# Three stages of a fused kernel: self attention with its products in another order, single-head attention with query and key on ScalarE, contexts in 128 rows

## What is computed

```python
x = x + L0_xattn(layernorm(x), ctx)     # 16 heads, cross
x = x + L0_ffn(layernorm(x))            # 8 experts, top 1
x = x + L1_xattn(layernorm(x), ctx)     # one head of width 128, cross
x = x + L1_ffn(layernorm(x))            # 15 experts, top 3, and a shared one
x = x + L2_xattn(layernorm(x), ctx, mask)   # 16 heads, masked
x = x + L2_ffn(layernorm(x))            # a whole block: causal self attention, then 8 experts
x = x + L3_xattn(layernorm(x), ctx)     # 8 heads of width 64
x = x + L3_ffn(layernorm(x))            # 8 experts with a capacity
```

```python
query = x @ Wq + bq; key = ctx @ Wk + bk; value = ctx @ Wv + bv
attended = softmax(query @ key.T / sqrt(128)) @ value
```

```python
q = rmsnorm(apply_rope(q, cos, sin), qn_w)      # the rms of 20 heads of 8
attn = softmax(where(causal, q @ k.T / sqrt(8), -inf)); out = attn @ v
out = out * sigmoid(out @ Wg + bg);  x = x + out @ Wo + bo
```

## Times and profile before

| | |
|---|---|
| median of 3 runs | 1868.89 us (1868.3 to 1873.9) |
| profiled execution | 1870.34 us, span 1868.5 us |
| mean granted TensorE clock | 0.909 of full speed |
| TensorE busy | 1506.6 us, 81% of the span |
| VectorE busy | 1329.3 us, 71% |
| ScalarE busy | 959.9 us, 51% |
| GpSimd busy | 860.5 us, 46% |

### The profile page before, as it was taken

How to read it: one execution, slowest core, us unless ns; L and a number is a source line. 1 busy time by engine, 2 the same in 40 slices (tenths; PEclk the granted TensorE clock), 3 DMA queues, 4 the chain that set the end, 5 groups by cost and what they waited for, 6 DMA issues and landing times. The chain is left out here.

```text
span 1868.5 us, 37548 instructions
## 1 busy us (share of the span) xinstructions
PE 1506.6 (81%) x11614; PEld 1169.2 (63%) x11614; DVE 1329.3 (71%) x4215; ACT 959.9 (51%) x1953; POOL 860.5 (46%) x1432
## 2 busy tenths in 40 slices
PE   5999949877898989788885888888768899999840
PEld 3666639865687777455553555555557798888630
DVE  4899943278777777688875888888556688887522
ACT  2788825433343333477773777777533344444310
POOL 2456643355110010233326777888544555665426
PEclk9999969978899999699985999999879899999965
DMA  6776118511000000000000000000066000000043
GB/s 200 234 267 236 36 36 258 161 39 33 5 1 1 1 1 1 7 9 9 9 2 1 1 2 1 6 7 8 16 182 198 14 15 13 21 21 18 12 149 89
DMA packets 60786, 108.35 MB, mean 58 GB/s; under 512 B 11715, under 2 KB 49620, under 8 KB 59796
## 3 DMA queue, kind: packets, MB, share of 16 engines
q1 hardware_dynamic: 54452, 93.45, 16.1%
q0 software_dynamic: 6144, 12.60, 2.3%
HBM read 89.49 MB, written 52.17 MB: 76 GB/s over the span
## 5 line engine op out<-in xcount | busy, mean ns | idle before, releaser
L716 DVE TENSOR_REDUCE parts<-PS 128x8 fp32r<-128x1024 f32 x192 | 234.1, 1219 | 42.4 <-PE PS L463 38.0
L954 ACT ACTIVATE P<-PS 128x1024 f32<-128x1024 f32 x192 | 198.3, 1033 | 71.7 <-PE PS L478 71.6
L931 ACT CAST qS<-PS 32x512 fp32r<-32x512 f32 x384 | 221.2, 576 | 6.8 <-PE PS L430 3.5
L1788 DVE SCALAR_TENSOR_TENSOR X<-PS,wt,X 128x128 f32 (+1 forms) x480 | 134.4, 344 | 49.5 <-PE PS L1631 40.9
L279 POOL TENSOR_TENSOR ve<-mv,eps_t 128x1 f32<-128x1 f32 x160 | 31.9, 199 | 283.3 <-DVE mv L275 282.9
L1920 ACT ACTIVATE P<-PS,w_f_b 128x512 f32<-128x512 f32 x128 | 88.0, 688 | 142.7 <-PE PS L1612 141.2
L1631 PEld LDWEIGHTS PS<-w_f_w,P 128*128 128x128 f32 x1024 | 130.4, 193 | 39.8 <-issue 27.9
L1631 PE MATMUL PS<-w_f_w,P 128*128 128x128 f32 x1024 | 142.4, 283 | 13.7 <-DVE X L1788 11.9
L478 PE MATMUL PS<-qS,kS 128*128 128x512 f32 x384 | 149.3, 444 | 1.0 <-ACT P L954 1.0
L430 PE MATMUL PS<-ident_r,parts 128*128 128x128 f32 x768 | 124.3, 293 | 30.7 <-issue 25.2
L845 POOL TENSOR_TENSOR rrs<-rsq,neg_half 128x20 f32<-128x20 f32 x32 | 115.2, 3600 | 46.4 <-DVE rsq L646 45.9
(11 more groups left out here) (302 smaller groups left out, 4332.4 us busy)
## 6 DMA issues: line engine op xcount, KB each, us to landing
P<-in_f_blob SPq DMA_DIRECT2D x12, 578.0 KB, 4.4
Y<-in_f_blob SPq DMA_DIRECT2D x11, 578.0 KB, 4.4
ctxT<-in_ctxT SPq DMA_DIRECT2D x128, 48.0 KB, 1.8
tok<-hs SPq DMA_DIRECT2D x46, 128.0 KB, 3.3
hs<-yo SPq DMA_DIRECT2D x46, 128.0 KB, 3.7
P<-in_f_blob SPq DMA_DIRECT2D x12, 450.0 KB, 4.3
Y<-in_f_blob SPq DMA_DIRECT2D x11, 450.0 KB, 4.7
w_f_w<-in_f_w SPq DMA_DIRECT2D x2, 1024.0 KB, 5.6
```

What stands on the lines that cost most here:

```text
L716: e.tensor_reduce(parts[:, it.s, 0, 8 * half:8 * half + 8, 3, 0], S_ps[:, :, :].rearrange("p i (j t) -> p (i j) t", t=T), AXX, ALU.max)\
L931: m = e.copy(qS[r, it.s % 2, :, j, :], TP[0][r, :].rearrange("p (g t) -> p g t", g=4))
L954: e.activation(P[:, it.s % 2, 8 * half:8 * half + 8, :].rearrange("p h t -> p (h t)"), ST_ps[:, :, :].rearrange("p j n -> p (j n)"), ACT.E ...
L1788: m = e.scalar_tensor_tensor(out=X_s, in0=rows, scalar=wt[:, b, s, x:x + 1], in1=X_s, op0=ALU.mult, op1=ALU.add)
```

## The change

Three edits stand together.

1. In the self attention VectorE does `v_heads` and `v_heads_back` ahead of `v_qk_norm`, and TensorE's order is `pe_stack_k`, `pe_scores(0)`, `pe_stack_q`.
2. In the single-head attention query and key leave PSUM on ScalarE (`a_qk`, at the head of its tick), the value alone on VectorE (`v_v`), from a bank of its own pair; `pe_qkv` waits for both, and GpSimd issues its gathers three ahead.
3. The context tile and the six context weights get 128 rows, of which the last 32 are zero (one memset of the tile, the weights padded on the host); the DMAs fill the first 96 rows of the tile as before.

```diff
-        weight("a1", "a1_wk", [C, D])
+        weight("a1", "a1_wk", [128, D])
...
-        ctxT = sb("ctxT", [C, RING, T])
+        ctxT = sb("ctxT", [128, RING, T])
...
-                        e.dma_start(ctxT[:, s, :], ctx_dram[:, 0, s, :]).then_inc(s_ctx[s], 16)
+                        e.dma_start(ctxT[0:C, s, :], ctx_dram[:, 0, s, :]).then_inc(s_ctx[s], 16)
...
                         if it := item(L + 1):
-                            pe_stack_q(e, it)
                             pe_stack_k(e, it)
                         if it := item(L):
                             pe_scores(e, it, 0)
+                        if it := item(L + 1):
+                            pe_stack_q(e, it)
...
-                        if it := item(F + 1):
-                            v_qk_norm(e, it)
                         if it := item(L + 3):
                             v_heads(e, it)
                             v_heads_back(e, it)
+                        if it := item(F + 1):
+                            v_qk_norm(e, it)
...
-            QKV = [FR, PS[:, 3, :]]
+            QK = [FR, PS[:, 3, :]]
+            V = [PS[:, 1, :], PS[:, 5, :]]
...
                     if due(it.n - 1):
                         e.wait_ge(s_v, at(s_v, it.n - 1))
-                    bank = QKV[it.s % 2]
+                        e.wait_ge(s_qk, at(s_qk, 2 * (it.n - 1)))
+                    bank = QK[it.s % 2]
...
-                    e.tensor_scalar(q1[:, it.s, :], bank[:, 0:T], w[p + "bq"][:, 0:1], None, ALU.add).then_inc(s_qk, 1)
-                    e.tensor_scalar(k1[:, it.s, :], bank[:, T:2 * T], w[p + "bk"][:, 0:1], None, ALU.add)\
-                     .then_inc(s_qk, 1)
-                    e.tensor_tensor(v1[:, it.s, :], bank[:, 2 * T:3 * T], w[p + "bv"][:, :], ALU.add).then_inc(s_v, 1)
+                    e.tensor_tensor(v1[:, it.s, :], V[it.s % 2][:, 0:T], w[p + "bv"][:, :], ALU.add).then_inc(s_v, 1)
...
-                    for i in range(2):
+                    for i in range(3):
                         pre["gather"](e, i)
                     for i in range(B):
-                        if i + 2 < B:
-                            pre["gather"](e, i + 2)
+                        if i + 3 < B:
+                            pre["gather"](e, i + 3)
...
+                def a_qk(it):
+                    if due(it.n - RING + 1):
+                        e.wait_ge(s_s, at(s_s, it.n - RING + 1))
+                    e.wait_ge(s_qkv, at(s_qkv, it.n + 1))
+                    bank = QK[it.s % 2]
+                    e.activation(q1[:, it.s, :], bank[:, 0:T], ACT.Identity, bias=w[p + "bq"][:, 0:1]).then_inc(s_qk, 1)
+                    e.activation(k1[:, it.s, :], bank[:, T:2 * T], ACT.Identity, bias=w[p + "bk"][:, 0:1])\
+                     .then_inc(s_qk, 1)
...
                 for item in unrolled(4 + lead):
+                    if it := item(2 + lead):
+                        a_qk(it)
                     if it := item(4 + lead):
                         a_pT(it)
...
+            e.memset(ctxT[C:128], 0.0).then_inc(consts_ready, 1)
```

More of the change, by code:

```diff
@@ L108, in build @@
         weight("a0", "a0_wq", [D, D])
-        weight("a0", "a0_wkv", [C, 2 * D])
+        weight("a0", "a0_wkv", [128, 2 * D])
         weight("a0", "a0_bqk", [T, 2 * D])
@@ L115, in build @@
         weight("a1", "a1_wq", [D, D])
-        weight("a1", "a1_wk", [C, D])
-        weight("a1", "a1_wv", [C, D])
+        weight("a1", "a1_wk", [128, D])
+        weight("a1", "a1_wv", [128, D])
         weight("a1", "a1_bq", [D, 1])
@@ L121, in build @@
         weight("a3", "a3_wq", [D, 512])
-        weight("a3", "a3_wk", [C, 512])
-        weight("a3", "a3_wv", [C, 512])
+        weight("a3", "a3_wk", [128, 512])
+        weight("a3", "a3_wv", [128, 512])
         weight("a3", "a3_wo", [128, 4, D])
@@ L126, in build @@
         weight("a2", "a2_wq", [D, D])
-        weight("a2", "a2_wkv", [C, 2 * D])
+        weight("a2", "a2_wkv", [128, 2 * D])
         weight("b2", "b2_wqkv", [D, 192])
@@ L247, in build @@
         consts_ready = sem("consts_ready")
-        N_CONSTS = 13
+        N_CONSTS = 14
         eps_ready = sem("eps_ready")
@@ L360, in sync @@
                             e.wait_ge(s_qkv, at(s_qkv, (g - 1) * RING + s + 1))
-                            e.dma_start(ctxT[:, s, :], ctx_dram[:, g, s, :]).then_inc(s_ctx[s], 16)
+                            e.dma_start(ctxT[0:C, s, :], ctx_dram[:, g, s, :]).then_inc(s_ctx[s], 16)
                         for i in range(3 * (g - 1), min(3 * g, 2 * NREG - 1)):
@@ L1059, in pe_qkv @@
                     e.matmul(bank[:, T:2 * T], w[p + "wk"][:, :], ctxT[:, it.s, :], start=True, stop=True)
-                    e.matmul(bank[:, 2 * T:3 * T], ctxT[:, it.s, :], w[p + "wv"][:, :], start=True, stop=True)\
+                    e.matmul(V[it.s % 2][:, 0:T], ctxT[:, it.s, :], w[p + "wv"][:, :], start=True, stop=True)\
                      .then_inc(s_qkv, 1)
@@ L1095, in vector, with v_v @@
             def vector(e):
-                def v_qkv(it):
+                def v_v(it):
                     if due(it.n - RING + 1):
@@ L1136, in vector @@
                     if it := item(2 + lead):
-                        v_qkv(it)
+                        v_v(it)
             def pool(e):
@@ L1173, in scalar @@
                 before(e)
+                e.wait_ge(sem(p + "weights"), 16 * n_loads[p[:2]])
                 for item in unrolled(4 + lead):
+                    if it := item(2 + lead):
+                        a_qk(it)
                     if it := item(4 + lead):
@@ L2658, in _ @@
             e.memset(ones[:], 1.0).then_inc(consts_ready, 1)
-            e.wait_ge(consts_ready, 3)
+            e.memset(ctxT[C:128], 0.0).then_inc(consts_ready, 1)
+            e.wait_ge(consts_ready, 4)
             for j in range(4):
@@ L2767, in layout @@
     a["zeros"] = np.zeros((REG * BLK, D), np.float32)
+    for name in ("a0_wkv", "a1_wk", "a1_wv", "a2_wkv", "a3_wk", "a3_wv"):
+        a[name] = np.pad(a[name], ((0, 128 - C), (0, 0)))
     return a
```

3 lines of the change are left out of this document (1 added, 2 removed).

## The result

The changed kernel took 1838.99 us (median of 4 runs, 1836.2 to 1839.9) beside 1868.6 us for the kernel before on the same chip: a ratio of 0.984, with an interval of 0.9825 to 0.9858, 29.6 us off. On a second chip it was 1838.06 and 0.9823 (0.9798 to 0.9848). The prediction was 1852 with a range of 1842 to 1863: the direction was right, the gain 1.7 times the 17 us forecast.

What follows compares the result with a forecast made beforehand. No engine was full; it saw single-head ticks bound by the gather loop, self attention by the power and VectorE's list with its hole, meeting closely. Self attention -4 and single-head -13 made -17 us: 1868.89 to 1852, range 1842 to 1863.

Steps and rivals of the forecast that it cites:

- Single-head: Single-head attention: tick falls from 2.97 to 2.31 us; 15.2 + 1.5 - 3.6 = 13 us gained, bounds 8.5 and 16.7.
- the leg of 1.20: Single-head loop of 2.31 us: the 1.20 us from VectorE's aggregate over GpSimd's root to the next normalization.
- the clock's: Single-head attention: four ticks at TensorE's slow clock cost 0.9 us each, 3.6 us taken off the gain.
- Self attention: Heads ahead of the power's product and scores between the stacks: 4 us gained, bounds 1 and 17.
- gained is what VectorE lacks now: Self attention, wait for the power before line 657: 0.09 us a tick, 2.4 us in some 27 ticks.
- Scores between the stacks: Self attention: key stack still waits for the residual, so nothing, except below 1 us together in a few late-`g_low` ticks.
- Rival (b): Self attention: the hole before the first maximum closes after all, 12.7 us more, 1839 us; chance 0.08.
- 128 rows: Context products: matmuls of 96 and 128 rows both take 275 ns, so nothing; any clock effect inside the single-head bounds.
- single-head bounds: Single-head gain from 8.5 us (as much slow clock time as before) to 16.7 us (none).
- (c): Single-head attention: landing of gathers still sets the tick, 2.97 us stays, 1865 us; chance 0.06.
- (d): Single-head attention: ScalarE sets the tick at 2.8 us, gain 4 us, 1861 us; chance 0.05.
- (e): Single-head attention: TensorE stays at 1.2 GHz for the whole stage, tick 3.3 us at most, 1876 us; chance 0.03.

Runs made afterwards that it cites:

- gathers_only: The kernel before with only the single-head gathers issued three ahead, query and key still on VectorE: 1855.55 us, ratio 0.9924.
- self_only: The kernel before with only the self attention's edits (heads ahead of the power's product, scores between the stacks): that stage took 339.5 us instead of 349.4.
- heads_only: The kernel before with only the self attention's heads moved ahead of the power's product: 1859.71 us, ratio 0.9952.
- residual_first: The changed kernel with VectorE's residual addition of the self attention moved ahead of the rotary step: 1836.33 us, ratio 0.9823.

## Why the prediction was wrong in size

The sum missed 12.6 us. By the stages of several traces some 3 of them are of the single-head attention (15.8 for 13), 5 of the self attention (8.7 for 4), and 5 lie outside both, where the prediction had put nothing.

**Single-head, forecast 13, measured 14 (11 to 18) alone and 15.8 by the stage (16.7 in the first pair of traces).** The loop held as described: the landing's wait gone, the leg of 1.20, a wait for the root in its place, ScalarE not the limit. The term taken too large was the clock's, 3.6 us for four slow ticks: the granted clock was 0.98 (and 1.00 in the second trace, 0.96 and 0.98 in others). One reading was wrong: from the last ticks the prediction took that VectorE isn't the limit "even with query and key on it". Those ticks have less of VectorE's work in them; in gathers_only, in full ticks with query and key on VectorE, its own list sets 2.52 us and the root makes it wait once, 0.3 us. The sum didn't suffer, since both edits came together.

**Self attention, forecast 4, measured 13 (8 to 17) alone and 5 to 10 by its stage (mean 8.7).** The failed step is "gained is what VectorE lacks now, 1208.49 - 1208.40 = 0.09 us". It stopped at the start of line 657 and took for granted that what follows lasts as long as before. Lines 657 and 664 were 0.16 and 0.14 us longer than their own time, because GpSimd's additions, which stand behind the power in its list, ran beside them; the net was 0.25 a tick instead of 0.09. Over 27 ticks that is 6.8 us in place of 2.4. A second gap was in the late ticks, of which I took one for all: they alternated between 9.89 and 10.72 us, on the mean 0.57 longer than after. From the eleventh tick on the stage's ticks took 215.9 us before and 207.2 after. Against this, the first ten took 97.1 us in the changed kernel (two of 11.5 and 11.1 us where 8.8 and 9.5 stood) and 93.2 in the kernel before, at granted clocks of 0.75 and 0.87 in those stretches. That is not shown to be due to the edit: the first ten took 94.1 to 97.1 us in five kernels with both edits and 93.2 to 95.4 in five with neither. Of self_only's trace 9.9 us lie in the stage and 5 ahead of it, where they can't be due to the edit.

**Scores between the stacks, forecast nothing:** right in the steady ticks, for the reason given (key stack 0.10 behind the residual, L460 0.47 behind it, hole of 0.94). In the late ticks it gave 0.1 to 0.2 us each, in some ten of them, where "below 1 us" in all was forecast. Rival (b) hit the number 1839 by luck: its hole did not close, and in the two runs in which it did, the whole was 1836 and 1842 us.

**128 rows, forecast nothing,** with the clock "inside the single-head bounds". That was too narrow a place: what they are worth, 1 to 7 us and not shown beyond the noise in any one pair, would lie elsewhere too, in part in the masked attention. The 4 us ahead of the single-head stage in the first profiled execution were absent in the second (0.3), so they are a difference between executions.

Of the rivals, (c), (d) and (e) are refuted for this kernel: no wait for gathered rows, ScalarE idle 14.4 us before its 27 first new operations (0.66 in the tick shown), clock 0.98. ScalarE's additions took 0.368 and 0.360 us where VectorE's took 0.319, off the loop. The Trainium skill's advice to keep additions on VectorE (ScalarE: Activation LUTs, Rules for kernel authors) could be passed over here without harm.

What stays open: why the clock is higher with 128 rows, and whether the 5 us outside the two stages are theirs; and why late ticks alternate when GpSimd's line 827 is late, beyond that they do.

## What to carry to other kernels

When two paths meet within a few hundredths of a microsecond, look past the meeting point: what the same event releases on the other engine runs beside the next lines, and their durations aren't constants. Compare the mean of each line with its shortest instance elsewhere in the trace; a line that lasts 0.48 us here and 0.32 there may have a neighbour on the other engine. Moving the neighbour helps only if it lands beside work that it doesn't lengthen (here the row maximum and the bias addition, which read PSUM), and if it pushes nothing else over other lines. After a stall goes, name the next two limits, each with an experiment that does one half of the edit: here landing 2.9, VectorE 2.5, root 2.3.

## What the runs showed of the hardware

A two-input VectorE operation on SBUF beside a 128x128 GpSimd addition or subtraction (0.46 us) lasted 0.14 to 0.27 us longer in the median: 0.32 to 0.48 (128x160), 0.29 to 0.43 (128x128), 0.23 to 0.50 (128x80). The row maximum (1.22 us) and the bias addition from PSUM (0.35 us) beside the same additions lasted no longer. Beside the power of 3.5 to 3.6 us line 737 kept its 0.22 us, and the normalization of line 676 its 0.34.

Two SBUF inputs aren't the whole condition, though. Operations with one were lengthened too: line 646 (20 columns) lasted 0.38 instead of 0.18 us beside line 826, in the late ticks of heads_only; line 654, a copy, 0.39 instead of 0.19 beside line 849 in the first ticks of the kernel before; line 677, a normalization, 0.53 instead of 0.34 beside line 850 in residual_first, once. Not lengthened were the reciprocal of line 726 (0.25 us) beside the additions in heads_only and the sum of squares of line 645 (0.32 us) beside line 826.

The same kernel's granted clock differed between executions by more than 0.01 on the mean (0.902 to 0.915 for the kernel before), with times from 1863 to 1873 us; where the clock changes, a difference of 4 us between two single traces needs no edit: the same kernel reached the single-head stage at 370.4 us in one execution and at 374.0 in another.
